# Row-tiled edge stage two image pairs ahead: start-up and engine orders re-done, and the edge sums of the third and fourth pair moved to GpSimd

## What is computed

```python
gray = einsum('bchw,c->bhw', x, (0.2989, 0.587, 0.114))
h = abs(conv(gray, scharr_x)) + abs(conv(gray, scharr_y)), halved
n = layernorm(h)
q, k, v = n @ Wq + bq, n @ Wk + bk, n @ Wv + bv        # q and k then times Wp per head
h = h + softmax(q k^T / 4) v
y = silu((layernorm(h) * gamma + beta) @ w1 + b1)
h = h + 0.5 * (y @ w2 + b2)
```

## Time and profile before

| | |
|---|---|
| median of three runs | 315.38 us |
| profiled execution, its own time | 317.39 us |
| its span, first to last instruction | 315.6 us |
| busy: PE, DVE, ACT, POOL | 284.4, 206.3, 173.8, 136.9 us |
| mean granted clock of PE | 0.961 |

### The profile page before, as it was taken

The page is one execution under the profiler, slowest core; times in us unless marked ns, Lnnn a source line. Parts: engine busy times, 40 slices in busy tenths (PEclk is TensorE's granted clock), DMA queues, the critical chain, the costliest instruction groups (busy, mean ns, idle before and its releaser), DMA issues.

```text
span 315.6 us, 6328 instructions
## 1 busy us (share of the span) xinstructions
PE 284.4 (90%) x2332; PEld 221.0 (70%) x2332; DVE 206.3 (65%) x415; ACT 173.8 (55%) x330; POOL 136.9 (43%) x268
## 2 busy tenths in 40 slices
PE   5599059889699998899999999999999999999996
PEld 5477047767577765666666666566899899899976
DVE  8586454855699988488889888662872742641432
ACT  2416476857063378377878768768444344344450
POOL 7250534531100014766286864217859489600000
PEclk9989759999999999599999999999999999999999
DMA  6828613178979794367568000000000200200201
GB/s 213 264 61 286 185 37 137 66 223 179 322 194 316 237 335 148 92 178 225 189 160 206 11 3 2 2 0 3 0 2 0 68 2 0 70 0 0 69 0 66
DMA packets 27310, 35.90 MB, mean 114 GB/s; under 512 B 5184, under 2 KB 16272, under 8 KB 27280
## 3 DMA queue, kind: packets, MB, share of 16 engines
q1 hardware_dynamic: 27184, 35.43, 37.3%
q10 hardware_dynamic: 96, 0.07, 0.1%
HBM read 24.42 MB, written 10.49 MB: 111 GB/s over the span
## 4 chain that ended last, share of the span: by engine, by line
PE 57%; DVE 9%; DMA 8%; ACT 7%; SPq 7%; POOL 5%; issue 4%; ACTq 1%; DVEq 0%; POOLq 0%
PE bank L1198 30%; PE bank L1327 7%; PE bank L1279 6%; PE bank L1302 4%; PE bank L1307 3%; PE bank L1345 3%; DMA bv<-in_L_attn_bv 3%; DVE negmax L909 3%; DMA wscale<-in_L_ffn_fc_scales 2%; SPq L427 2%; DMA halo_x<-in_x 2%; SPq L417 2%; PE bank L1216 1%; ACT xn L1083 1%; PE bank L1337 1%
## 5 line engine op out<-in xcount | busy, mean ns | idle before, releaser
L909 DVE TENSOR_REDUCE negmax<-bank 128x2 f32<-128x512 f32 x128 | 82.1, 684 | 6.9 <-PE bank L1279 6.6
L1109 ACT ACTIVATE probs<-bank 128x512 f32<-128x512 f32 x128 | 66.3, 603 | 29.1 <-PE bank L1307 29.1
L963 DVE TENSOR_TENSOR y_l<-yf,y_h 128x512 fp32r<-128x512 f32 x32 | 24.1, 754 | 38.6 <-ACT yf L1135 38.4
L1132 ACT ACTIVATE y_h<-bank,b1col 128x512 fp32r<-128x512 f32 x32 | 22.0, 687 | 47.7 <-PE bank L1198 47.6
L1198 PE MATMUL bank<-w_h,y_h 128*128 128x256 f32 x128 | 36.9, 289 | 1.1 <-DVE y_l L963 0.7
L1198 PE MATMUL bank<-w_l,y_h 128*128 128x256 f32 x128 | 36.2, 283 | 0.0
L1198 PE MATMUL bank<-w_h,y_l 128*128 128x256 f32 x128 | 36.2, 283 | 0.0
L1327 PE MATMUL bank<-probs,vals 128*32 128x256 f32 x512 | 35.1, 393 | 0.0
L1279 PE MATMUL bank<-ks,qs 48*128 48x256 f32 x256 | 32.6, 333 | 1.3 <-DVE negmax L909 0.7
L1279 PEld LDWEIGHTS bank<-ks,qs 48*128 48x128 f32 x256 | 19.8, 189 | 15.1 <-DVE negmax L909 6.1
L1307 PEld LDWEIGHTS bank<-qs,ks 48*128 48x128 f32 x256 | 24.9, 189 | 2.7
(11 more groups left out here) (158 smaller groups left out, 609.7 us busy)
## 6 DMA issues: line engine op xcount, KB each, us to landing
xr<-in_x SPq DMA_DIRECT2D x8, 768.0 KB, 8.5
qs<-qk_parts SPq DMA_DIRECT2D x48, 128.0 KB, 3.2
ks<-qk_parts SPq DMA_DIRECT2D x48, 128.0 KB, 3.3
qk_parts<-qk_h SPq DMA_DIRECT2D x16, 256.0 KB, 3.1
qk_parts<-qk_l SPq DMA_DIRECT2D x16, 256.0 KB, 3.2
wraw<-in_L_ffn_fc_q SPq DMA_DIRECT2D x4, 512.0 KB, 5.0
wscale<-in_L_ffn_fc_scales SPq DMA_DIRECT2D x4, 512.0 KB, 6.8
out<-osb SPq DMA_DIRECT2D x16, 128.0 KB, 1.8
```

The source lines that it names most:

```text
L909: eng.tensor_reduce(negmax[:, b % 2, u, v], entry_bank(key)[:, :].rearrange("p (t k) -> p t k", t=NT), AX.X, ALU.max, negate=True).then_in ...
L963: eng.tensor_tensor(y_l[:, p % 2, f], yf[:, n % 2], y_h[:, p % 2, f].bitcast(fp32), ALU.subtract).then_inc(s_y, 1)
L1109: eng.activation(probs[:, n % PBUF], p2[n % 4][:, :], ACT.Exp).then_inc(s_exp, 1)
L1132: eng.activation(y_h[:, p % 2, f], src, ACT.Silu, bias=b1col[:, f:f + 1])
```

## The change

The same work is computed. What moves:

- **Start.** On ACT and DVE the gray of image 1 goes ahead of the first border rows. PE's filler transposes ahead of the first `tok` are 12 instead of 8.
- **SP.** Images 4 and 5 are loaded ahead of the second border rows; the wait for the cleared `halo` moves to the second `stack_halo`.
- **POOL.** `tok_rstd(0, t)` goes ahead of the split of the v weights, which waits for a DMA.
- **ACT and DVE between.** `halo_scale(1)`, `halo_add(1)`, `gray_scale(4)`, `halo_high(1)` go behind `tok_normalise(0, 0)` and others; `edge(1, 0)` is cut into its two halves; the preparation of `pick` goes behind the whole stage on DVE.
- **Pairs 2 and 3.** `edges` leaves DVE; POOL gets `add_edges(p, t)` ahead of `tok_rstd(p, t)`. ACT's `edge(p + 2, 1)` and DVE's `tok_moments(p + 2, 1)` go further back.
- **Banks.** The banks of `turns` are dealt out anew; `xt(0)` now uses banks 0 and 1, and so PE waits for the folded weights (`s_wready`) ahead of `xt(0)` instead of behind it.

```diff
-        fold_over, heads_begin = turn["qkv", 0, 0], turn["qkv", 1, 5]
+        fold_over, heads_begin = turn["xt", 0, 0], turn["qkv", 1, 5]
-            if fold_over <= n < heads_begin:
-                r = (0, 1, 2, 3, 6, 7, 4, 5)[(n - fold_over) % 8]
+            if n < fold_over:
+                r = 4 + n % 4
+            elif n < heads_begin:
+                r = (0, 1, 2, 3, 4, 5, 6, 7)[(n - fold_over) % 8]
             else:
-                r = 4 + (n if n < fold_over else n - heads_begin) % 4
+                if n == heads_begin:
+                    upper = sorted(range(4, 8), key=lambda q: turn[uses[q][-1]])
+                r = upper[(n - heads_begin) % 4]
...
+            def add_edges(p, t):
+                wait_read(eng, ("tok", p, 2 * t))
+                wait_read(eng, ("tok", p, 2 * t + 1))
+                h = hid[:, p, t].rearrange("p b e -> p (b e)")
+                eng.tensor_tensor(h, h, absd[:, t], ALU.add).then_inc(s_edges, 1)
...
             gray_add(0)
-            halo_add(0)
             gray_low(0)
             gray_add(1)
+            halo_add(0)
+            gray_low(1)
             halo_low(0)
-            gray_low(1)
...
             def tok_stats(p, t):
-                edges(p, t)
+                if p < 2:
+                    edges(p, t)
                 tok_moments(p, t)
...
-            gray_scale(4)
-            halo_scale(1)
             tok_normalise(0, 0)
-            halo_high(1)
-            edge(1, 0)
+            halo_scale(1)
+            edge(1, 0, (0,))
             tok_normalise(0, 1)
+            gray_scale(4)
             for kf in range(KE):
                 xt_high(0, kf)
+            halo_high(1)
             gray_scale(5)
+            edge(1, 0, (1,))
             edge(1, 1)
...
-                    if i in TOK_AT and p + 2 < PAIRS:
-                        edge(p + 2, TOK_AT.index(i))
-                        if p == 0 and i == TOK_AT[0]:
+                        if p == 0:
                             gray_scale(6)
-                    if i == XT_AT and p + 1 < PAIRS:
+                    if i == 1 and p + 2 < PAIRS:
+                        edge(p + 2, 0)
+                    if i == 3 and p + 1 < PAIRS:
                         for kf in range(KE):
                             xt_high(p + 1, kf)
                         if p == 0:
                             gray_scale(7)
+                    if i == 3 and p + 2 < PAIRS:
+                        edge(p + 2, 1)
...
-            keep_busy(8, bank[0])
+            keep_busy(12, bank[0])
...
+            eng.wait_ge(s_wready, 4)
             for kf in range(KE):
                 xt(0, kf)
-            eng.wait_ge(s_wready, 4)
```

More of the change, by code:

```diff
@@ L453, in _ @@
             stack_halo(eng, 0)
-            eng.wait_ge(s_halo_z, 2)
+            load_x(4)
+            load_x(5)
             load_halo(eng, 1)
-            load_x(4)
             eng.dma_start(wv_src[:], Wv.rearrange("(k p) n -> p k n", p=P)).then_inc(s_wld, 16)
-            load_x(5)
             for t in range(NT):
@@ L699, in _ @@
                 gray_low(b)
+            for t in range(NT):
+                tok_rstd(0, t)
             eng.wait_ge(s_wld, 16 * (NT + 1))
@@ L702, in _ @@
             eng.tensor_tensor(wqk_l[:, :, 2 * E:], wv_src[:], wqk_h[:, :, 2 * E:].bitcast(fp32), ALU.subtract).then_inc(s_wvready, 1)
-            for t in range(NT):
-                tok_rstd(0, t)
             for b in range(4, 6):
@@ L710, in _ @@
             for t in range(NT):
-                tok_rstd(2, t)
                 gray_high(6 + t)
                 gray_low(6 + t)
+                add_edges(2, t)
+                tok_rstd(2, t)
             for t in range(NT):
+                add_edges(3, t)
                 tok_rstd(3, t)
@@ L841, in _ @@
                 eng.tensor_copy(wtr[:, op], bank[op][:, :]).then_inc(s_wtc, 1)
-            eng.wait_ge(s_ident, 1)
-            link(eng.tensor_reduce(picked[:], ident[:].rearrange("p (v c r u) -> p u v c r", v=2, c=8, r=2)[:, :, :, 0], AX.XY, ALU.add))
-            eng.tensor_copy(pick[:], picked[:]).then_inc(s_pick, 1)
             def weights(op):
@@ L974, in tok_stats @@
             def tok_stats(p, t):
-                edges(p, t)
+                if p < 2:
+                    edges(p, t)
                 tok_moments(p, t)
             tok_stats(0, 0)
-            halo_add(1)
             tok_stats(0, 1)
@@ L982, in _ @@
                 weights(op)
-            halo_low(1)
+            halo_add(1)
             gray_add(4)
@@ L986, in _ @@
                 xt_low(0, kf)
+            halo_low(1)
             gray_add(5)
@@ L995, in _ @@
                         tok_stats(1, 1)
-                    if i in TOK_AT and p + 2 < PAIRS:
-                        if p == 0 and i == TOK_AT[1]:
-                            gray_add(6)
-                        tok_stats(p + 2, TOK_AT.index(i))
-                    if i == XT_AT and p + 1 < PAIRS:
+                    if (p, i) == (0, 1):
+                        gray_add(6)
+                    if i == 1 and p + 2 < PAIRS:
+                        tok_stats(p + 2, 0)
+                    if i == 3 and p + 1 < PAIRS:
                         for kf in range(KE):
@@ L1004, in _ @@
                             gray_add(7)
+                    if i == 4 and p + 2 < PAIRS:
+                        tok_stats(p + 2, 1)
+            eng.wait_ge(s_ident, 1)
+            link(eng.tensor_reduce(picked[:], ident[:].rearrange("p (v c r u) -> p u v c r", v=2, c=8, r=2)[:, :, :, 0], AX.XY, ALU.add))
+            eng.tensor_copy(pick[:], picked[:]).then_inc(s_pick, 1)
             for s in range(END):
@@ L1065, in halo_high, with edge @@
                 eng.activation(halo_hl[0:24, g], halo_g[:, g], ACT.Copy).then_inc(s_halo_h, 1)
-            def edge(p, t):
-                for half in range(2):
+            def edge(p, t, halves=range(2)):
+                for half in halves:
                     key = ("tok", p, 2 * t + half)
@@ L1140, in _ @@
             gray_high(0)
+            gray_scale(1)
             halo_scale(0)
-            gray_scale(1)
+            gray_high(1)
             halo_high(0)
-            gray_high(1)
             gray_scale(2)
```

5 lines of the change are left out of this document (3 added, 2 removed).

## The result

The changed kernel takes 301.91 us (median of four runs, 301.36 to 303.05); the kernel before took 315.2 us beside it (314.59 to 318.14). The ratio is 0.9565, with a 95% interval from 0.9499 to 0.9631: 13.3 us less, where 12.5 were forecast. The profiled execution of the changed kernel took 301.64 us, with a span of 299.9 us and a mean granted clock of PE of 0.989 (before: 315.6 us of span, 0.961). PE is busy 281.1 us of it (284.4 before), DVE 204.8, ACT 173.2, POOL 141.9. So of the 15.7 us by which this span is shorter, 12.4 are idle time of PE that is gone (31.2 before, 18.8 after), and the other 3.3 are busy time of PE.

A forecast was written before the change was run, and what follows sets the result against it. PE's idle time ahead of 90 us, then a fixed 64.0 us chain from SP's first read-back, was taken as the bound; the read-back coming 12.5 us earlier gave 315.4 - 12.5 = 302.9 us, range 300.0 to 307.0.

The forecast's parts named there:

- The start: Beginning, up to the first edge: `tok(0)` at 13.3 instead of 16.25, `edge(0, t)` at 19.7 instead of 22.80, 3.1 us won.
- The gap of PE: PE's 9.62 us wait for `xn` ahead of `xt(0)`: `xt(0)` at 29.3 instead of 41.60, 12.3 us won.
- From `xt(0)` to `qkv(0, 0)`: Stage behind the gap: `qkv(0, 0)` starts at 32.7 instead of 45.04, 12.3 us earlier.
- PE's clock: PE between 10 and 50 us: short waits don't lower the clock, PEclk near 1.00.
- The edge sums on POOL: Sums moved from DVE: 1.28 us each on POOL; DVE stands from 44.0 to 47.3; last `qk_l` of pair 0 at 49.8.
- Pair 1: Second pair: `qk_l(1, 3)` made at 65.9, SP wants to store it at 67.5, 1.6 us of cover.
- The chain of 64.0 us: Fixed stretch from SP's first read-back to PE's `negsplit`: 51.8 of issues, 7.4, 4.8; the end moves with the read-back.
- Late transfers: Rival, 14 of 100: border rows of `load_halo(1)` land at 30.2, `xt(0)` starts 3.6 us later, time 306.5.
- POOL's sums holding up pair 1 so far that SP waits: Rival, 10 of 100: pair 1's chain slips over 1.6 us, SP waits for `qk_l(1, 3)`, time 305.
- The half clock at 127 us going: Rival, 12 of 100: PE's half clock from 127.40 to 134.38 goes, 2.7 us more won, time 300.2.
- Slower by a clock that stays low: Rival, 2 of 100: PE's new short waits keep it at 1.2 GHz; 318 if held up to pair 2.
- PE bound by DVE, so that it comes no earlier than before: Rival, 2 of 100: SP's first read-back moves, but PE stays bound by DVE behind it, time 313 to 316.

The follow-up runs named there:

- a_start: Changed kernel with the beginning's old order (border rows ahead of gray of image 1, eight fillers): 305.44 us, ratio 0.9705.
- b_start: Kernel before with only the new beginning (gray of image 1 ahead of the border rows, 12 fillers): 314.12 us, ratio 0.9991.
- b_pool: Kernel before with only `tok_rstd(0, t)` moved ahead of the v weights on POOL: 308.16 us, ratio 0.9784.
- a_wvlate: Changed kernel with POOL's two operations on the v weights moved behind `tok_rstd(1, t)`: 301.51 us, ratio 0.9581.
- a_same: The changed kernel unaltered, run and profiled once more beside other runs: 302.25 us, ratio 0.9592.
- a_dve: Changed kernel with the edge sums of pairs 2 and 3 back on DVE, none on POOL: 301.53 us, ratio 0.9558.
- a_all: Changed kernel with all edge sums on DVE, v weights behind `tok_rstd(1, t)` on POOL, and a later first feed-forward weight step: 299.88 us, ratio 0.9522.
- a_sp: Changed kernel with SP's old order, the second border rows ahead of images 4 and 5: 302.51 us, ratio 0.9589.
- b_w1: Kernel before with POOL's feed-forward weight steps beginning at slot 10 of the attention loop instead of 6: 314.35 us, ratio 0.9981.

## Why the prediction was right

**The start: right.** `tok(0)` was forecast at 13.3 and starts at 13.35, at full clock; DVE ends `gray_low(1)` at 13.20, as worked out. The first edge was forecast at 19.7 and starts at 19.24. That its 3.1 us count was right for this kernel only: a_start gives 3.2 to 3.5 us, b_start nothing that can be measured.

**The gap of PE: right.** POOL ends the second `tok_rstd` at 27.58 (forecast 27.8), `xt(0)` starts at 29.54 (29.3) with 0.76 us of waiting ahead (forecast under 1). The split was 3.1 by the start, 1.9 by DVE's order and the rest (7.3) by POOL's. At `xt(0)` itself, from 41.60 by b_pool (35.66) and a_start (32.51) to 29.54, it is 5.9 by POOL's order, 3.2 by all else, and 3.0 by the start; no run has DVE's order alone.

**From `xt(0)` to `qkv(0, 0)`: a term mis-sized.** Forecast 32.7, measured 33.54. I costed `halo_add(1)` by its usual rows, 0.41 us each, in a place where POOL now works on the v weights. It took 2.2 us instead of 0.8, which a_wvlate takes away. DVE's low part of the border rows lost another 0.5 us behind `xt_low`, beside `gray_l`.

**PE's clock: partly wrong.** I expected PE's short waits not to lower the clock. Behind the wait of 2.94 us, PE goes at 1.2 GHz from about 34 to 37.5 us, as the row at 34.46 shows (0.63 us; the first one, at 33.54, takes 0.47). It cost nothing at SP's queue: PEclk between 30 and 40 us is 0.83 in the changed kernel and 0.66 in a_same, and their first read-backs stand at 51.70 and 51.69.

```profile
30.00:40.00 10.00, 7.24 (x27) 5.29 (x27) 9.63 (x19) 7.44 (x14) 6.43 (x9) 0.66 0.53 144
```

That is the row of a_same. That `tok(2, 0)` starts at 38.41 instead of 36.7 isn't the clock's doing: it waits for POOL's `gray_l`, which ends at 38.27 because DVE ends `gray_add(5)` at 35.80 instead of 34.4, by the stretched rows of the term before.

**The edge sums on POOL: right in kind, 0.6 us off.** The sum was forecast at 1.28 us, by the subtraction, and takes 1.28 to 1.30. DVE waits 3.16 us for it (forecast 3.3). The last `qk_l` of pair 0 is done at 50.4 instead of 49.8 and the read-back starts at 51.70 instead of 50.85. The Trainium skill ("GPSIMD Engine Reference", section 4.1, Engine selection) says that two-input elementwise work is about twice as slow on GpSimd; the trace agrees: 1.28 us against 0.69. The waiting of DVE was in my sum, with a sum at 47.3 that DVE alone could have had by 45.7; what that costs at the end I didn't work out. Taken back in the changed kernel they bring nothing that can be told from none (a_dve, 0.7 us); taken back in a_wvlate, with the later weight step, 1.6 us (a_all). So this part of the change gained nothing, and most likely lost something.

**Pair 1: right.** Its `qk_l(1, 3)` was forecast at 65.9 and ends at about 66.1; SP stores from 67.82 on (forecast 67.5), with no gap.

**The chain of 64.0 us: there, but shorter, and not alone in setting the end.** From SP's first read-back to PE's row at `negsplit` it is 63.3 us in a_same, where PE waits for it until 115.00 (forecast 114.9), and 62.4 in the profile after, where PE doesn't wait at all. To POOL's first weight step it was 59.2 us in the profile before and is 57.5 in the profile after, 58.5 in a_same; the issues from the first read-back to `wscale` alone took 50.8 us and now take 49.1 and 49.5. Two of the signs that I named failed in the profile after: POOL's wait for `wscale` is 2.62 us instead of 4 to 5 (4.40 in a_same), and PE's for `negsplit` isn't there (1.58 in a_same).

I moved the end by the read-back's 12.5 us. The read-back moved by 11.7 and the time by 13.3, so what lies behind the read-back became 1.6 us shorter, which I had at nothing. That the sum is only 1.0 us off is in part luck: the read-back is 0.85 us later than forecast, and the shorter rest more than makes up for it. What became shorter there is at least the queue's 1.3 to 1.7 us of issues and PE's 3.06 us of waiting at 81.28, now 1.74 at 67.93. ACT's 1.73 us for the stores of pair 2 are gone in the profile after, but a_same has such waits of ACT, of up to 4.70 us, and is hardly slower. These are read from the profiles; no run takes them apart.

**The rivals.** Late transfers: refuted, by ACT's row at 26.78 and by a_sp. POOL's sums holding up pair 1 so far that SP waits: not seen. The half clock at 127 us going: it is gone in the profile after, but b_w1, without the wait, is at most 1.5 us faster than before, so little or nothing was won by it; how often the usual execution of before has it isn't known. Slower by a clock that stays low: it came, for 3 us in the profile after and for longer in a_same (PEclk 0.66), and recovered. PE bound by DVE, so that it comes no earlier than before: refuted by the result, with PE at `negsplit` at 114.11 instead of 127.40.

## What to carry to other kernels

In an in-order engine, look for the instruction that waits for a late DMA while others behind it have their inputs: moving eight small instructions past it was worth 7 us of 13, and until that was done the faster beginning was worth nothing that could be measured. When a sum or a copy is moved to another engine, its own length is the smaller part of the price; count what it stands behind there, and what the old engine then waits for (3.2 us for 1.28 of work). To know whether a queue or an engine carries the end, delay the queue alone by a few microseconds of dummy work: one such run says more than a dozen in which all moves together. And profile the same kernel twice: here one execution is held by the queue and the other isn't, at nearly the same time.
